# Two attention blocks on one core: first and last iterations rebuilt, and a middle with another order of TensorE's work

## The reference

```
# layer 0: x is (channels 256, tokens 512); 8 heads of 32; keys and values are the query
q = x^T @ Wq^T
logits = (q q^T / sqrt(32) * cmask + (1 - cmask) * -1e30) * rmask      # mask of keys, mask of rows
x = x + transpose((softmax(logits) @ q) @ Wo^T)
# layer 1: the 256 channels are now the tokens, 512 features, 16 heads of 32
scale, shift = split(cond @ W_emb + b_emb)
xn = rms_norm(x) * g_norm * (1 + scale) + shift
q, k, v = split(xn @ W_qkv);  q = rms_norm(q) * g_q;  k = rms_norm(k) * g_k      # per head
o = softmax(q k^T / sqrt(32)) @ v
x = x + o + o @ W_out
```

## Time and profile before

| | us |
|---|---|
| median of three runs | 1330.34 |
| lowest, highest | 1325.32, 1330.52 |
| the profiled execution's own time | 1324.62 |
| its span | 1322.8 |

### The profile page before, as it was taken

One profiled execution on the slowest core, in us unless ns is written; L12 is line 12 of the kernel. 1 busy time (PEld: TensorE's weight loads), 2 busy tenths in 40 slices (PEclk: granted clock), 3 DMA queues, 4 the chain that ended last, 5 costly groups with the idle time before them and its releaser, 6 DMA issues.

```text
span 1322.8 us, 20986 instructions
## 1 busy us (share of the span) xinstructions
PE 1261.4 (95%) x6896; PEld 597.6 (45%) x6896; DVE 1055.8 (80%) x934; ACT 774.6 (59%) x1377; POOL 764.4 (58%) x389
## 2 busy tenths in 40 slices
PE   6969899999999999999999999999999999999987
PEld 4424444444444454444445444444444444444433
DVE  6756778888887887888788788878888887888654
ACT  1626565665656566565656666565666656566523
POOL 0337467475746747484674748467474856638452
PEclk8859899999999999999999999999999999999999
DMA  8321534525264452626445252634525263441322
GB/s 288 105 65 47 136 105 96 140 54 151 74 148 109 99 138 56 149 72 150 107 107 131 60 147 70 153 104 112 130 60 145 69 156 100 113 110 44 97 59 70
DMA packets 77962, 143.03 MB, mean 108 GB/s; under 512 B 21536, under 2 KB 23072, under 8 KB 77856
## 3 DMA queue, kind: packets, MB, share of 16 engines
q1 hardware_dynamic: 69136, 126.17, 38.1%
q10 hardware_dynamic: 8720, 15.51, 4.0%
HBM read 32.02 MB, written 8.39 MB: 31 GB/s over the span
## 4 chain that ended last, share of the span: by engine, by line
PE 88%; ACT 4%; DVE 2%; issue 2%; SPq 1%; ACTq 1%; POOL 1%; DMA 0%; DVEq 0%
PE PX L541 25%; PE PS L453 11%; PE PO L480 9%; PE PX L575 8%; PE PO L502 5%; PE PS L467 4%; PE PX L398 4%; PE PM L422 4%; PE PX L519 2%; PE PM L491 2%; PE PM L519 2%; PE PM L559 2%; PE PM L431 2%; PE PO L505 2%; ACT E L1055 2%
## 5 line engine op out<-in xcount | busy, mean ns | idle before, releaser
L1048 ACT ACTIVATE E<-PS,KBIAS 128x512 f32<-128x512 f32 x512 | 345.3, 686 | 236.8 <-PE PS L453 221.9
L541 PE MATMUL PX<-WQKV,XNT 128*128 128x512 f32 x768 | 382.4, 602 | 3.4 <-ACT QK L1026 2.1
L1948 POOL TENSOR_TENSOR E<-E 128x1024 f32<-128x1024 f32 x112 | 263.4, 2359 | 160.8 <-PE PO L480 92.9
L1565 DVE TENSOR_REDUCE NM<-PM 128x4 f32<-128x2048 f32 x128 | 291.3, 2276 | 52.3 <-PE PM L422 52.3
L453 PE MATMUL PS<-B,A 97*128 97x512 f32 x512 | 301.7, 624 | 5.3 <-ACT E L1048 4.9
L1978 POOL TENSOR_TENSOR KQLO<-E 128x1024 f32<-128x1024 f32 x64 | 151.2, 2363 | 211.3 <-ACT E L1055 209.5
L1960 POOL TENSOR_TENSOR RQK<-RQK,HALF 128x16 f32<-128x16 f32 x64 | 201.0, 3148 | 28.3 <-DVE RQK L1653 27.5
L1572 DVE TENSOR_REDUCE NM<-PM 128x8 f32<-128x2048 f32 x64 | 146.6, 2291 | 49.1 <-PE PM L431 49.0
L541 PEld LDWEIGHTS PX<-WQKV,XNT 128*128 128x128 f32 x768 | 137.8, 192 | 91.4 <-issue 75.7
L1055 ACT ACTIVATE E<-PS 128x512 f32<-128x512 f32 x256 | 145.3, 596 | 49.0 <-PE PS L467 48.3
L453 PEld LDWEIGHTS PS<-B,A 97*128 97x128 f32 x512 | 95.6, 192 | 148.1 <-issue 123.6
(11 more groups left out here) (84 smaller groups left out, 1408.2 us busy)
## 6 DMA issues: line engine op xcount, KB each, us to landing
A<-QHI SPq DMA_DIRECT2D x256, 64.0 KB, 2.0
B<-QHI SPq DMA_DIRECT2D x256, 64.0 KB, 2.0
A<-KQHI SPq DMA_DIRECT2D x128, 128.0 KB, 2.3
B<-KQHI SPq DMA_DIRECT2D x128, 128.0 KB, 2.4
XB<-x SPq DMA_DIRECT2D x16, 512.0 KB, 3.9
A<-QLO SPq DMA_DIRECT2D x128, 64.0 KB, 2.0
B<-QLO SPq DMA_DIRECT2D x128, 64.0 KB, 2.0
X<-x ACTq DMA_DIRECT2D x16, 512.0 KB, 5.4
```

Of the source, the lines that this page charges most:

```text
L541: last = mm(PX[:, :], XNT[:, c, t * P:(t + 1) * P], WQKV[:, c, part * DM:(part + 1) * DM], start=(c == 0), stop=(c == 3))
L1048: fn(E[:, probs(seg, i, g), h, :], PS[n % 2][:, :], ACT.Exp, bias=KBIAS[:, g, b:b + 1], scale=SCALE).then_inc(exp_done, 1)
L1565: v.tensor_reduce(NM0[:, q, :].rearrange("p (h k) -> p h k", k=KB0)[:, :, kb], PM[:, :, :], axis=AX.X, op=ALU.max, negate=True).then_inc(m ...
L1948: g_.tensor_tensor(running(seg, i)[:, heads_, :], running(seg, i)[:, heads_, :], E[:, probs(seg, i, g), heads_, :], ALU.add).then_inc(done, 1)
```

## The change

- The mask moves behind the projection. TensorE projects the raw x; ScalarE's copy to QF sums the rows as it goes (`accum_out`, into QSUM); GpSimd multiplies QF by the mask (`mask_query`). `sums_x`, `mask_x`, `project_mean` and `mean0` are gone. CBI now holds (1 - mask)/512.
- `modulation` moves from iteration -1 to iteration 0, behind the fourth maxima group of segment B. W_emb has a buffer of its own (in the space of a later tile), its result goes to PX.
- The weights are loaded by SP in four DMAs with a semaphore each, W_emb and Wo behind the first stack, W_qkv and W_out at the end of SP's list for iteration -1. ScalarE issues four of the eight stacks of the first sample.
- The middle's lists are reordered: scores stand in twos, and groups of row and column tiles are put next to each other.
- Iteration 16: `qk` alternates between PX and bank 3 of PM; VectorE scales the heads; ScalarE issues two of the four stacks; the row of maxima goes out in two halves (`rows1_half`), the first after two of the four maxima groups.
- Iterations 0 and 15 are reordered too.

```
-            def project_mean(i, b):
-                big(("mean", 0), i)
-                ...
+                pe.wait_ge(xin_in.sem, xin_in.at(b))          # project0, was xm_done
...
-                copy(QF[:, mt, :], PX[:, :]).then_inc(big_taken, 1)
+                fn(QF[:, mt, :], PX[:, :], ACT.Copy, accum_out=QSUM[:, mt, b:b + 1]).then_inc(big_taken, 1)
...
+            def mask_query(i, b, mt):
+                pool.wait_ge(cbm_in.sem, cbm_in.at(b))
+                pool.wait_ge(big_taken, BIG.upto(("p0", mt), i))
+                g_.tensor_tensor(QF[:, mt, :], QF[:, mt, :], CBM[:, :], ALU.mult).then_inc(masked.sem, 1)
...
+            def rows1_half(i, b, j):                          # TensorE
+                pe.wait_ge(context_taken, CONTEXT_TAKEN.ahead(("n1", j), i))
+                pe.wait_ge(max_done, MAXES.upto(("c", 2 * j + 1), i, QUAD))
+                tp(PO[0:H1, j * P:(j + 1) * P], NM1[:, j * H1:(j + 1) * H1], IDENT[:, :]).then_inc(n1_half[j], 1)
...
+        def heads_bank(b, k):
+            return PM[:, 3, :] if b == NB - 1 and k % 2 else PX[:, :]
...
             def iteration_before(i):                          # SP
-                stack0(i + 1, 0, 3)
-                stack0(i + 1, 0, 1)
                 stack0(i + 1, 0, 0)
+                load_modulation()
                 load_x(i + 2)
                 stack0(i + 1, 0, 2)
-                stack0(i + 1, 1, 3)
                 stack0(i + 1, 1, 2)
                 stack0(i + 1, 1, 0)
-                stack0(i + 1, 1, 1)
+                load_weights()
...
             def iteration_16(i):                              # ScalarE
                 round_heads(i, i - 1, 3)
+                stack1(i, i - 1, 3)
+                stack1(i, i - 1, 1)
+                rows1_half(i, i - 1, 0)
                 values1(i, i - 1, 0)
-                rows1(i, i - 1)
                 exp1(i, i - 1, 0, 0)
```

More of the change, by code:

```diff
@@ L70, in place @@
     def place(self, key):
-        return next(where for k, _, where in self.uses if k == key)
+        return next(where for uses in (self.uses, *self.special.values()) for k, _, where in uses if k == key)
 QUAD = "quad"
@@ L250, in cond_resid @@
         A1 = sb("A1", [P, QH, Q1, N1], F32R)
+        with nc.sbuf_tensor("WEMB", [P, 4, 2 * DM], F32) as WEMB:
+            pass
         B1 = sb("B1", [P, QH, Q1, N1], F32R)
@@ L326, in cond_resid @@
         n1_full = ev("n1_full", 1)
+        n1_half = [sem(f"n1_half{j}") for j in range(2)]
+        row1_half_in = [sem(f"row1_half_in{j}") for j in range(2)]
         row1_in = ev("row1_in", 16)
@@ L367, in _ @@
             mm, tp = nc.tensor.matmul, nc.tensor.transpose
-            def modulation(n):
-                if n == 0:
-                    pe.wait_ge(mod_in.sem, 16 * 3)
-                    pe.wait_ge(ct_in.sem, 16)
-                for c in range(4):
-                    last = mm(PO[:, n * NB:(n + 1) * NB], WEMB[:, c, n * P:(n + 1) * P], CT[:, c, :],
-                              start=(c == 0), stop=(c == 3))
-                if n == 7:
-                    last.then_inc(mod_full.sem, 1)
             def small(key, i):
@@ L384, in small, with modulation @@
                 return PM[:, k, :]
+            def modulation(i):
+                big(("mod", 0), i)
+                pe.wait_ge(mod_in.sem, 16 * 3)
+                pe.wait_ge(ct_in.sem, 16)
+                for n in range(8):
+                    for c in range(4):
+                        last = mm(PX[:, n * NB:(n + 1) * NB], WEMB[:, c, n * P:(n + 1) * P], CT[:, c, :],
+                                  start=(c == 0), stop=(c == 3))
+                last.then_inc(mod_full.sem, 1)
             def quad_free(key, i):
@@ L540, in project1 @@
                 for c in cs:
-                    last = mm(PX[:, :], XNT[:, c, t * P:(t + 1) * P], WQKV[:, c, part * DM:(part + 1) * DM],
+                    last = mm(bank, XNT[:, c, t * P:(t + 1) * P], WQKV[:, c, part * DM:(part + 1) * DM],
                               start=(c == 0), stop=(c == 3))
@@ L1107, in take_heads @@
                     act.wait_ge(tq_full.sem, tq_full.at(b - 1))
[L1108 removed]
+                copy(QK[:, k // 2, (k % 2) * DM:(k % 2 + 1) * DM], heads_bank(b, k)) \
+                    .then_inc(bank_taken[3] if b == NB - 1 and k % 2 else big_taken, 1)
             def square_heads(i, b, k):
@@ L2106, in stack1 @@
                 sp.wait_ge(score_full, SCORES.upto(("C", 15), b))
-                own = slice(hq * DH, (hq + 1) * DH)
-                stack(A1[:, hq, :, :], B1[:, hq, :, :], KQHI[own, 1, :, :], KQLO[own, 1, :, :],
-                      KQHI[own, 0, :, :], KQLO[own, 0, :, :], stack1_in[hq])
+                for dst, src in stack1_rows(hq):
+                    sp.dma_start(dst, src).then_inc(stack1_in[hq].sem, 16)
             def store(i, b):
```

821 lines of the change are left out of this document (422 added, 399 removed), and 23 rows, old and new, of tables (BIG, special).

## The result

| | before | after |
|---|---|---|
| median, us | 1330.34 (7 runs, 1321.93 to 1331.37) | 1320.43 (7 runs, 1316.04 to 1323.50) |
| ratio after / before | | 0.9944, 95% interval 0.9919 to 0.9969 |
| the profiled execution, and its span | 1324.62, 1322.8 | 1322.51, 1320.4 |

The account below looks back on a forecast made before the run. The prediction took three stages with limits of their own: ramp, TensorE-bound middle, end. From the profiled 1324.62 us, -18.5 (middle), -2.0 (ramp) and -6.0 (end) gave 1298.1, plus 2 for run offset: 1300, range 1285 to 1317.

Parts of the forecast that it names:

- What bounds the kernel: Whole kernel: a ramp of 100 us, a middle with TensorE busy 986.34 of 1000 us, an end with DMA engines at 0.80.
- The middle: Fourteen iterations: mean projection removed and tile groups put side by side save 1.32 us each, 18.5 in all, between 5 and 24.
- Scores by twos: Middle: placing scores in pairs was priced at nothing, at most 0.2 us an iteration.
- rivals 3 and 4: Middle: 3, savings return as waits for exponentials, 1319, 6%; 4, pairs of scores starve, slower, 1358, 6%.
- Out 6.85, in 6.9: nothing: Ramp: modulation leaves the way to the first score, 6.85 us, and returns in iteration 0 at full clock, 6.9: no net change.
- the 2.0 of the ramp: Ramp: summed terms gave a gain of 2.0 us, from 9 us faster to 5 us slower.
- First score near 33: Ramp: sign that the forecast is right, the first score starting near 33 us, where it was 36.69.
- The clock is low where TensorE has holes: Ramp: reading of the trace said to agree with the skill's rule that sustained activity releases the throttled clock.
- The end: Last sample: two stack issuers and a halved maxima row bring the third score earlier, gain 6.0 us, between 1 and 10.
- from there to the last store nothing is shorter: End: from the last sample's third score to the last store no time is gained.
- Rival 2: Ramp and end: the ends give nothing, modulation at low clock (+6.8), stacks bound by DMA engines (-1 for -6); 1312, 13%.
- Rival 3: Middle: TensorE's savings come back as waits for exponentials, only the ends' 8 us are left; 1319, 6%.

Follow-up runs that it names:

- e3: Changed kernel with the old order of the fourteen middle iterations, without row sums and mean projection, query mask behind the projection: 1341.01 us, ratio 1.0105.
- e2: Changed kernel with 24 filler products of 256 columns added in iteration -1, modulation left in iteration 0: 1321.54 us, ratio 0.9960.
- e1: Changed kernel with the modulation back in iteration -1, in pieces behind the maxima groups, W_emb issued by ScalarE: 1304.39 us, ratio 0.9837.
- e5: Changed kernel with x loaded ahead of W_emb and iteration 0's first four scores ahead of the next sample's projection: 1322.39 us, ratio 0.9970.
- e9: e5's order of first scores, with the row of maxima behind only segment A's stacks on ScalarE, large weights after its landing: 1319.69 us, ratio 0.9956.
- e4: Changed kernel with iteration 16's maxima row issued by SP, its first copy ahead of ScalarE's second stack, the store last: one run, 1315.16 us.
- e8: e4 with iteration 16's stacks issued from ScalarE, GpSimd and SP, and two value-projection passes ahead of the first score: one run, 1314.55 us.
- e10: Changed kernel with e2's filler and only 16 of the modulation's 64 products, three quarters of its sum left out: one run, 1312.48 us.

## Why the prediction was wrong, step by step

- **What bounds the kernel: right.** Three stages with limits of their own, and each went its own way.
- **The middle: right in kind.** The busy part fell by 1.36 an iteration, forecast 1.32; its two steps, 0.98 and 0.34, measured 0.86 and 0.50 (e3). I left the idle time unchanged; it grew by 0.29, one wait for GpSimd's scaling. So fourteen iterations gain 15.0 and not 18.5; the stage of the table, with iteration 15, gains 16.5. Scores by twos brought no wait for exponentials (rivals 3 and 4 are out).
- **"Out 6.85, in 6.9: nothing" is the step that failed.** Two errors. The price: I took the modulation at full clock; it took 13.83 at the low one, and 11.5 where it started at the full (e2). The 24 products in 3.19 us that spoke for the full clock were the first to run: the granted clock was 1.00 up to 20 us and 0.74 from 20 to 22. The credit: the 6.85 us did not stand alone on the way to the first score. The row's transfer stood beside it. Before, it landed 3.6 us after its issue at 29.80, at 33.4, so without the modulation no more than 3.3 us were to be had; now it landed after 7.1 us, and the first score is at 36.57 as before. The prediction also contradicts itself here: a first score near 33 is a gain of 3.7 in all, not 6.85 beside the 2.0 of the ramp. In iteration -1 the products filled waits for the maxima, in iteration 0 they stand between scores. e1 shows both at once: 16 us.
- **"First score near 33": wrong by 3.5 us.** The copy of the row came at 29.05, 1.5 us behind the 27.5 that I had worked out. The sum of the ramp has no term for the landing, and the text does not work the 33 out. The DMA engines were full from 22 to 42 us with W_emb, x, stacks and weights in one stretch, and in e5 the row, issued at 29.86, held TensorE until 37.52, 7.7 us. With the queue kept free and 12 issues fewer ahead of the row (e9) the first score is at 27.16.
- **"The clock is low where TensorE has holes": the rows did not say that.** Before, TensorE is busy all the time from 26 to 36 us at half clock, and in the first 20 us it is busy 9.46 us at 1.00:

```profile
26.00:36.00 10.00, 10.00 (x50) 10.00 (x50) 3.66 (x6) 1.07 (x3) 0.00 (x0) 0.50 0.78 207
```

- **The end: two terms failed.** The half row was to be there 12.8 us after the first stack issue (16 issues of 0.68, and 1.9 to land); it took 16.85. ScalarE's 12 issues take 10.2 us, 0.85 each with the queue full, the four of the half row 3.22, the landing 3. e4 takes them off ScalarE and gets 5.8 us back at the first score. And "from there to the last store nothing is shorter" left out what is longer, 4.4 us: six more passes of the value projection stand behind the first score, the second half row's issues between exponentials, and the clock is at 0.50 there; how the 4.4 divide is not measured. The 14.4 us of transfers that I took as the floor for the stacks are 15.9 to 16.0 in e4 and e8, and the third score came 18.8 us after the first issue.
- **Rival 2 was the nearest** (the modulation at the low clock, the ends give nothing, 1312 at 13%). It priced the block rightly but kept my credit for the first score, and no loss at the end. Rival 3's number, 1319, is nearer to the measured 1320.43, but by luck: its mechanism, waits for exponentials in the middle, did not come.

What is not settled: what lowers TensorE's clock near 50 us (e10 speaks against the small products as the cause), and why the same ramp code starts its second iteration at 111.9, 112.3, 108.4 and 107.8 in the changed kernel, e3, e4 and e8. The clock goes with it: from 44 to 50 us it is 0.50 in the changed kernel and 1.00 in e4, and the modulation takes 13.83, 13.84, 11.85 and 10.85 us in the four. So some 4 us of the ramp's +12.2 can come from the execution that was profiled, and the gain of the single runs e4 and e8 is not to be read from their totals.

## What to carry to other kernels

Work that fills a wait is free only there: before it is moved, ask what it displaces at the new place, and price it at the clock that the new place shows, not at that of its own first part. A transfer's landing time depends on what is queued in front of it (the row's 8 KB took 3.6 us before and 7.1 now): list the bytes that are issued ahead of it on all queues, also for the small ones, since a mask of 256 KB behind 4 MB cost TensorE 11.5 us. An instruction that issues transfers holds up its engine's list: look at which copy or exponential stands behind it.

## What was not expected of the hardware

- The half clock stays with a TensorE that records no idle time: from 50 to 64 us of the changed kernel it is busy 2.00 of every 2 us at 0.50. The Trainium skill ("TensorE: Matmul & The Clock Gate", Part 1) has activity release the throttle; in this stretch the trace disagrees, if a full record of small products counts as activity.
- A product of 16 columns starts 0.112 us behind the one before at full clock and 0.213 at half: at full clock that is the time of 128 columns (a pass of 512 took 0.43) for 16. The weight loads, one of 128 columns for each pass, are busy 13.73 of the block's 13.83 us, so it looks as if they and not the 16 columns set the pace. 0.213 x 64 is 13.6 of the 13.8 us.
- Issuing a transfer does not always take the same time: ScalarE's stack issues took 0.55 to 0.83 us each from 1273.5 to 1275.5 us of the changed kernel and 1.3 each from 1278.5 to 1281, where the DMA engines were full (1.06). But in the ramp, from 22 to 30 us, they were as full (1.05) and an issue took 0.5 to 0.7. So full engines alone do not explain it; what does stays open.
